# Dense queries and keys for the cross attention, and the delta rule's lower block applied to the scores

## What is computed

```python
# B=32 sequences, S=128 tokens, D=256.  x = LN(x + A(x)); x = LN(x + X(x, ctx)); x = LN(x + F(x))
# A: gated delta rule (4 key heads, 8 value heads of 128) and a mixture of 8 experts
q, k, v, z = split(zrms(x, w_ln1) @ W_qkvz)          # 512, 512, 1024, 1024 columns
beta = sigmoid(b); g = -exp(A_log) * softplus(a + dt_bias)
q, k, v = split(silu(causal_dwconv([q, k, v], conv_w)))   # 4 taps, q and k scaled to length 1
def step(S, inp):                                    # over the 128 tokens, per value head
    S = S * exp(gt)
    delta = (vt - kt @ S) * bt
    S = S + outer(kt, delta)
    o = qt @ S
core = rmsnorm(o) * gate_norm_w * silu(z)
h = x + core @ W_out
A(x) = h + sum over the 2 best of 8 experts of route * (silu(n @ Wg) * (n @ Wu)) @ Wd, n = zrms(h, w_ln2)
# X: cross attention, 16 heads of 16, over 128 context rows of the same sequence
scores = einsum('bnlh,bnph->bnlp', heads(x @ Wq.T + bq), heads(ctx @ Wk.T + bk)) / 4
scores = where(mask, scores, -1e8)
X(x, ctx) = (softmax(scores) @ heads(ctx @ Wv.T + bv)) @ Wo.T + bo
# F: 16 columns of 64 neurons, a gate that keeps one column, projection, layer norm
```

## Time and profile before

| | |
|---|---|
| median of 3 runs | 2331.67 us (2329.76 to 2333.71) |
| the profiled execution | 2329.89 us |
| its span | 2327.9 us |
| busy PE / PEld / DVE / ACT / POOL | 2219.2 / 1901.7 / 1678.1 / 1404.4 / 768.9 us |
| mean granted TensorE clock | 0.984 |
| DMA | 30.75 MB, nearly all of it in the first 40 us |

### The profile page before, as it was taken

One profiled execution on the slowest core, in us unless ns is written; L12 is line 12 of the kernel. 1 busy time (PEld: TensorE's weight loads), 2 busy tenths in 40 slices (PEclk: granted clock), 3 DMA queues, 4 the chain that ended last, 5 costly groups with the idle time before them and its releaser, 6 DMA issues.

```text
span 2327.9 us, 82936 instructions
## 1 busy us (share of the span) xinstructions
PE 2219.2 (95%) x33994; PEld 1901.7 (82%) x34026; DVE 1678.1 (72%) x5322; ACT 1404.4 (60%) x4326; POOL 768.9 (33%) x1771
## 2 busy tenths in 40 slices
PE   5899999999999999999999999999999999999986
PEld 4788888888888888888888888888888888888875
DVE  4577777777777777777777777777777777777753
ACT  3576555776555776555776555776555776555742
POOL 2332324333324332324332324333323333324321
PEclk8899999999999999999999999999999999999997
DMA  6000000000000000000000000000000000000000
GB/s 221 7 2 10 9 10 9 9 2 10 10 9 9 9 2 9 10 9 9 9 2 9 10 10 9 9 2 10 9 10 9 9 2 9 10 9 9 7 4 3
DMA packets 25065, 30.75 MB, mean 13 GB/s; under 512 B 8529, under 2 KB 21857, under 8 KB 23921
## 3 DMA queue, kind: packets, MB, share of 16 engines
q1 hardware_dynamic: 24688, 25.46, 3.3%
HBM read 21.25 MB, written 4.19 MB: 11 GB/s over the span
## 4 chain that ended last, share of the span: by engine, by line
PE 55%; DVE 22%; ACT 18%; issue 4%; POOL 1%; DVEq 0%; POOLq 0%
PE bank_b L644 10%; PE bank_a L460 6%; PE bank_b L736 5%; PE bank_b L652 5%; DVE acc L1010 4%; PE bank_a L542 4%; DVE diag L1046 3%; PE bank_b L673 3%; DVE y1p L1140 3%; DVE u L1087 3%; PE bank_a L581 3%; PE bank_a L572 3%; ACT prob L923 2%; ACT acc L814 2%; PE bank_a L532 2%
## 5 line engine op out<-in xcount | busy, mean ns | idle before, releaser
L1010 DVE SCALAR_TENSOR_TENSOR acc<-ypad,convw,acc 128x128 f32<-128x128 f32 x1536 | 432.2, 349 | 73.0 <-ACT acc L814 72.7
L460 PEld LDWEIGHTS bank_a<-xnT,wqkvz 128*128 128x128 f32 x2048 | 242.6, 195 | 43.3 <-DVE u L1087 42.8
L460 PE MATMUL bank_a<-xnT,wqkvz 128*128 128x128 f32 x2048 | 258.9, 281 | 17.1 <-DVE u L1087 17.1
L911 ACT ACTIVATE y1T<-bank_b 128x256 f32<-128x256 f32 x32 | 12.3, 384 | 313.0 <-PE bank_b L666 313.0
L1417 POOL TENSOR_SCALAR lnv<-mv 128x1 f32<-128x1 f32 x128 | 31.1, 243 | 509.5 <-DVE mv L1101 506.9
L923 ACT ACTIVATE prob<-bank_b,nmax 128x128 f32<-128x128 f32 x512 | 179.7, 374 | 2.2 <-DVE nmax L1160 1.8
L814 ACT ACTIVATE acc<-bank_a,convw 128x128 f32<-128x128 f32 x512 | 149.4, 405 | 0.0
L1321 POOL TENSOR_TENSOR gate<-ba,dtb 128x8 f32<-128x8 f32 x32 | 6.5, 203 | 430.3 <-ACT ba L825 430.3
L1158 DVE TENSOR_REDUCE smax<-bank_b 128x4 f32<-128x512 f32 x128 | 87.8, 686 | 68.5 <-PE bank_b L683 68.5
L736 PEld LDWEIGHTS bank_b<-y2T,wc 128*128 128x128 f32 x1024 | 124.3, 195 | 14.4 <-issue 14.4
L903 ACT ACTIVATE prob<-bank_b 128x512 f32<-128x512 f32 x64 | 38.2, 597 | 160.1 <-PE bank_b L644 160.1
(11 more groups left out here) (244 smaller groups left out, 5845.3 us busy)
## 6 DMA issues: line engine op xcount, KB each, us to landing
xin<-in_x_dram SPq DMA_DIRECT2D x32, 128.0 KB, 2.1
cin<-in_ctx_dram SPq DMA_DIRECT2D x32, 128.0 KB, 2.1
out_dram<-yout SPq DMA_DIRECT2D x32, 128.0 KB, 2.9
wqkvz<-in_wqkvz_dram SPq DMA_DIRECT2D x6, 512.0 KB, 6.8
wout<-in_wout_dram SPq DMA_DIRECT2D x1, 1024.0 KB, 9.8
wg<-in_wg_dram SPq DMA_DIRECT2D x1, 1024.0 KB, 11.4
wu<-in_wu_dram SPq DMA_DIRECT2D x1, 1024.0 KB, 13.4
wd<-in_wd_dram SPq DMA_DIRECT2D x1, 1024.0 KB, 15.2
```

Source lines behind the costliest of these rows:

```text
L460: last = mm(A[bank][:, b * P:(b + 1) * P], wqkvz[:, c, o:o + P], xnT[:, c, :], start=(c == 0), stop=(c == KC - 1))
L1010: stt(acc[:, c, :], ypad[:, c, k:k + P], convw[:, c, k:k + 1], acc[:, c, :], ALU.mult, ALU.add).then_inc(conv.sem, 1)
```

## The change

1. `q` and `k` are laid out dense: two heads share 32 rows, 128 rows hold 8 heads, so 2 blocks in place of 4. The keys stay in four blocks `kT`, in which `madj` (now 0 or 1 times mask) leaves one head of each pair and sets the other's rows to zero. Scores are 8 products with 256 moving columns (two key blocks side by side).
2. The mask row goes. Each score bank first gets `fill_bf` through a bf16 product with the identity, 512 columns, and the scores are added to it. POOL makes `madj` and `fill_bf` in three instructions where one was.
3. `a_w` and its DVE subtraction go. `a_mt` has 16 products where it had 8: the second set multiplies the lower inverse with the lower block of the scores. ACT writes the first result into `zfull` (negated), DVE the second into `scoreT` (`a_low`). `a_sz` now waits for both, ACT copies only its upper 64 rows back to `scoreT`, and `a_o` uses `scoreT`.
4. The arrays in DRAM stay padded. SP gathers the dense weights: 16 DMAs for `wq` and `wk` (128 partitions, 4 pieces of 16 floats each) and 32 for `bq` and `bk` (16 partitions, one float each), behind the 8 of `wo`; the four plain loads go. All count for `W_B`.
5. All four lists of `ORDER` are new.

```diff
-    put("mask_row", (p % 32 == HD) * -1.0)
+    put("parity", (p % 32 // HD == np.arange(2)[None, :]) * 1.0)
...
+    pe="b_v@2 b_x2T@2 a_lb01@1 a_la10@1 b_router@2 b_gu0@2 b_gu1@2 a_la11@1 a_lb10@1 b_gu2@2 a_la20@1 "
+       "a_lb11@1 b_gu3@2 b_dn0@2 a_lb20@1 a_la21@1 b_dn1@2 a_lb21@1 a_vT0@1 a_la30@1 b_k@2 a_la31@1 a_lb30@1 "
+       "a_lb31@1 b_y1T@2 a_pa@1 b_q@2 a_pb@1 c_s a_mt@1 c_pT0 a_vT1@1 a_xT a_sz0@1 c_pT1 a_ba a_qkv0 c_pT2 "
+       "a_o0@1 a_sz1@1 c_pT3 a_qkv1 a_o1@1 c_pv c_R a_z0 a_z1 c_xo a_qkv2 a_qkv3 c_y2T a_dec0 c_h a_ss c_lg "
+       "c_c0 a_st c_c1 c_wT a_kk c_spread a_dec1 c_pj0 b_oT0 b_oT1 c_pj1 b_w0 b_w1 a_la00 b_cT a_qk a_la01 "
+       "a_lb00".split(),
+    act="b_sum@2 b_cT@2 b_x2T@2 b_sg0@2 b_rl@2 b_sg1@2 b_rt@2 a_mix2@1 a_mix3@1 a_sum b_y1T@2 a_zf@1 b_q@2 "
+       "a_zo@1 c_exp0 a_mt@1 c_exp1 a_xT c_exp2 a_sz0@1 c_exp3 a_ba a_qkv0 a_o0@1 a_sz1@1 c_pT0 c_pT1 a_qkv1 "
+       "a_o1@1 c_R a_ln a_z0 a_mix0 a_z1 a_seg a_mix1 a_sq c_y2T c_h a_qkv2 a_st c_lt a_qkv3 c_c0 c_te c_wT "
+       "c_c1 a_dec0 a_dec1 b_oT0 b_oT1".split(),
+    dve="a_lb31@1 a_pa@1 b_k@2 a_u0@1 c_y4@3 c_max0 c_max1 a_xn c_max2 a_low@1 a_u1@1 c_max3 c_pT0 a_conv00 "
+       "a_conv01 c_pT1 a_conv02 c_rec a_core0@1 a_conv10 c_ao a_conv11 a_core1@1 c_sum2 a_conv12 c_y2 c_lb "
+       "c_route a_conv20 a_ss c_gc0 c_weight c_gc1 a_lower a_init c_sum3 b_hid a_la00 c_y3 b_x2 a_la01 "
+       "a_lb00 a_conv21 b_v a_conv22 a_lb01 a_conv30 a_la10 a_conv31 a_la11 a_lb10 b_act0 b_top a_conv32 "
+       "a_la20 a_lb11 a_score b_act1 b_ys0 a_la21 a_lb20 b_ys1 a_lb21 a_la30 a_la31 b_y1 a_lb30".split(),
+    pool="c_y2b@3 a_rq@1 c_ln2@3 b_xh@2 b_rs@2 b_rd@2 b_rt@2 c_ln3@3 a_xr@1 b_ln0@2 b_y1b@2 a_x a_osc0@1 a_ga "
+       "a_osc1@1 a_g c_ln1 c_rx b_mask c_sig a_sc".split(),
...
-        wq = sb("wq", [P, KC, 4 * P])
-        wk = sb("wk", [P, KC, 4 * P])
+        wq = sb("wq", [P, KC, 2 * P])
+        wk = sb("wk", [P, KC, 2 * P])
...
-        szT = decay
-        carryT = gseg[0:64, :, 0:64]
...
+        madj = sb("madj", [P, 2, P])
+        fill_bf = sb("fill_bf", [P, P], BF16)
...
+        dense_qk = [(w[:, :, P * o:P * o + P].rearrange("p k (j c d) -> p k j c d", j=4, c=2)[:, i, :, c, :],
+                     w_d.rearrange("p k (a j t) -> p k a j t", a=4, j=4, t=32)[:, i, 2 * o + c, :, 0:HD])
+                    for w, w_d in ((wq, wq_d), (wk, wk_d)) for i in range(KC) for o in range(2) for c in range(2)]
+        dense_b = [(b[32 * j + HD * c:32 * j + HD * c + HD, o:o + 1], b_d[32 * j:32 * j + HD, 2 * o + c:2 * o + c + 1])
+                   for b, b_d in ((bq, bq_d), (bk, bk_d)) for j in range(4) for o in range(2) for c in range(2)]
         W_A = 16 * (len(loads_a) + len(small_a))
-        W_B = 16 * (len(loads_b) + len(small_b) + len(dense_wo))
+        W_B = 16 * (len(loads_b) + len(small_b) + len(dense_wo) + len(dense_qk) + len(dense_b))
...
-            for dst, src in small_b + dense_wo:
+            for dst, src in small_b + dense_wo + dense_qk:
                 sp.dma_start(dst, src).then_inc(w_b.sem, 16)
+            for dst, src in dense_b:
+                sp.dma_start(dst, src, allow_slow_non_contiguous=True).then_inc(w_b.sem, 16)
...
-                    pe.wait_ge(*w_ok(n - 1, 1))
+                    pe.wait_ge(*carry_ok(n - 1))
...
-                    pe.wait_ge(*(w_ok(n - 1, 2) if g == 0 else core_ok(n - 1, 4 - g)))
+                    pe.wait_ge(*(lower_ok(n - 1) if g == 0 else core_ok(n - 1, 4 - g)))
...
             def a_mt(n):
+                pe.wait_ge(*score_ok(n))
                 pe.wait_ge(*zfull_ok(n)).then_inc(pe_passed.sem, 1)
                 for h in range(HV):
-                    last = mm(A[0][TOP, 64 * h:64 * h + 64], zfull[TOP, h, TOP], kkT[TOP, h, BOT], start=True, stop=True)
+                    part = slice(64 * h, 64 * h + 64)
+                    mm(A[0][BOT, part], kkT[TOP, h, BOT], zfull[TOP, h, TOP], start=True, stop=True)
+                    last = mm(A[3][BOT, part], zfull[BOT, h, BOT], scoreT[BOT, h, BOT], start=True, stop=True)
                 last.then_inc(carry_ps.sem, 1)
 
-            def solve_w(n, half):
+            def score_z(n, half):
                 pe.wait_ge(*carry_ok(n))
+                pe.wait_ge(*lower_ok(n))
                 pe.wait_ge(*u_ok(n, 1 + half)).then_inc(pe_passed.sem, 1)
-                for b in range(4):
-                    h = 4 * half + b
-                    last = mm(A[(0, 3)[half]][BOT, b * P:(b + 1) * P], carryT[:, h, :], u[TOP, h, :], start=True, stop=True)
-                last.then_inc(w_ps.sem, 1)
-
-            def score_z(n, half):
-                pe.wait_ge(*zfull_ok(n))
-                pe.wait_ge(*score_ok(n))
-                pe.wait_ge(*u_ok(n, 1 + half))
                 for b in range(4):
                     h = 4 * half + b
                     last = mm(A[1 + half][:, b * P:(b + 1) * P], zfull[:, h, :], scoreT[:, h, :], start=True, stop=True)
                 last.then_inc(sz_ps.sem, 1)
 
             def read(n, half):
-                pe.wait_ge(*sz_ok(n, 1 + half))
-                pe.wait_ge(*w_ok(n, 1 + half))
+                pe.wait_ge(*sz_ok(n, 1 + half)).then_inc(pe_passed.sem, 1)
                 for b in range(4):
                     h = 4 * half + b
-                    last = mm(A[1 + half][:, b * P:(b + 1) * P], szT[:, h, :], u[:, h, :], start=True, stop=True)
+                    last = mm(A[1 + half][:, b * P:(b + 1) * P], scoreT[:, h, :], u[:, h, :], start=True, stop=True)
                 last.then_inc(o_ps.sem, 1)
...
             def b_k(n):
                 pe.wait_ge(*ysum(n, 2))
-                for b in range(4):
+                for b in range(2):
...
             def b_q(n):
                 pe.wait_ge(*y1T_ok(n))
-                for b in range(4):
+                for b in range(2):
...
             def c_s(n):
-                pe.wait_ge(*q_ok(n))
-                pe.wait_ge(*k_ok(n))
-                for b in range(4):
+                pe.wait_ge(*madj_ok(n))
+                for j in (0, 2, 1, 3):
+                    if j == 1:
+                        pe.wait_ge(*k_ok(n))
+                    if j == 3:
+                        pe.wait_ge(*q_ok(n))
+                    mm(quad(Bk[j]), ident_bf[:, :], fill_bf[:, :].unsqueeze(1).to_broadcast([P, 4, P]), start=True, stop=False)
+                for o in range(2):
                     for j in range(4):
                         r = slice(32 * j, 32 * j + 32)
-                        last = mm(Bk[j][:, b * P:(b + 1) * P], qT[r, b, :], kT[r, b, :], start=True, stop=True)
-                        if b == 3:
+                        last = mm(Bk[j][:, D * o:D * o + D], qT[r, o, :], kT[r, 2 * o:2 * o + 2, :], start=False, stop=(o == 1))
+                        if o == 1:
                             last.then_inc(s_ps.sem, 1)
...
             def a_sq(n):
                 act.wait_ge(*mixed_ok(n, 2))
+                if not first(n):
+                    act.wait_ge(*o_ps(n - 1))
                 fn(sqk[:, :, :], mixed[:, 0:QK_BLOCKS, :], ACT.Square).then_inc(sq_ok.sem, 1)
...
                 act.wait_ge(*carry_ps(n))
-                fn(carryT, A[0][TOP, :].rearrange("p (h c) -> p h c", c=64), ACT.Copy).then_inc(carry_ok.sem, 1)
+                fn(zfull[BOT, :, TOP], A[0][BOT, :].rearrange("p (h c) -> p h c", c=64), ACT.Copy, scale=-1.0).then_inc(carry_ok.sem, 1)
 
             def score_z(n, half):
                 act.wait_ge(*sz_ps(n, 1 + half))
-                fn(heads(szT, half), quad(A[1 + half]), ACT.Copy).then_inc(sz_ok.sem, 1)
+                fn(scoreT[TOP, 4 * half:4 * half + 4, :], quad(A[1 + half])[TOP, :, :], ACT.Copy).then_inc(sz_ok.sem, 1)
...
                 act.wait_ge(*q_ps(n))
-                for b in range(4):
+                for b in range(2):
...
-            def solve_w(n, half):
-                dve.wait_ge(*w_ps(n, 1 + half))
-                tt(u[BOT, 4 * half:4 * half + 4, :], u[BOT, 4 * half:4 * half + 4, :], quad(A[(0, 3)[half]])[BOT, :, :],
-                   ALU.subtract).then_inc(w_ok.sem, 1)
+            def a_low(n):
+                dve.wait_ge(*carry_ps(n))
+                nc.vector.tensor_copy(scoreT[BOT, :, BOT], A[3][BOT, :].rearrange("p (h c) -> p h c", c=64)).then_inc(lower_ok.sem, 1)
...
                 dve.wait_ge(*madj_ok(n))
                 for b in range(4):
-                    last = stt(kT[:, b, :], Bk[1][:, b * P:(b + 1) * P], bk[:, b:b + 1], madj[:, :], ALU.add, ALU.mult)
+                    o, c = b // 2, b % 2
+                    last = stt(kT[:, b, :], Bk[1][:, o * P:(o + 1) * P], bk[:, o:o + 1], madj[:, c, :], ALU.add, ALU.mult)
...
             def b_mask(n):
+                if not first(n):
+                    pool.wait_ge(*s_ps(n - 1))
                 pool.wait_ge(*m_loaded(n)).then_inc(pool_passed.sem, 1)
-                ts(madj[:, :], m_u8[:, :], con("mask_row"), None, ALU.add).then_inc(madj_ok.sem, 1)
+                for c in range(2):
```

(2 more changed lines are left out.)

34 lines of the change are left out of this document (10 added, 24 removed), and 8 rows, old and new, of tables (dve, pe).

## The result

The kernel with the change took 2308.4 us (median of 7 runs, 2303.1 to 2319.6), the kernel before beside it 2329.8 (2327.9 to 2333.7): ratio 0.9907, interval 0.9885 to 0.9928. It is faster, by 21 us where 47 were forecast. The profiled execution took 2305.4, its span 2303.6, so the spans differ by 24.3.

The account below looks back on a forecast made before the run. PE, busy 95% of the span, was taken as the bound. 2329.9 - 73.6 (32 periods, 2.3 us each) + 24.8 (start) = 2281.1, which with 1.8 to the median gave 2283 us; forecast's own range 2267 to 2312, whole range 2245 to 2320.

Parts of the forecast that it names:

- PE's work: PE's steps per period: -3.95 removed, +0.84 fills, +0.30 a_mt, scores unchanged; sum -2.81 us, between -4.15 and -0.85.
- The waits: PE's idle time per period under the new orders: 0.8 + 0.3 - 0.6 = +0.5 us, period falling 2.3 to 67.9.
- (1): Behind the scores: c_pT0 waits for ACT's exponentials with only a_mt (about 1.4) ahead; up to 1.0 us idle, 0.8 taken.
- (2): Ahead of b_y1T: expert sum and normalisation need 4.2 us, filler is 3.7; idle 0.5 against 0.2.
- (3): At a_qkv2: it waited 0.49 us for a_core through a chain mostly on ACT; 0.5 of idle left as is.
- 0.6 of old gaps: Smaller old PE gaps that the new list closes, taken off the added idle: 0.6 us a period.
- The start: Once, at trip 2: PE stands until the last gathered weight or bias lands, 70.5 - 45.7 = 24.8 us; bounds 14 and 70.
- Rival (a): At the start: gather pieces cost 0.125 us each or more; 2329 us, no gain, or 2393 at twice that; chance 0.04.
- (c): The start is cheap, 14 us down to 7; time 2265 to 2272 us; chance 0.16.
- (e): Scores of 256 columns lose row-group overlap; 2325 us at half the loss, 2366 at all; chance 0.02.
- (d): New order closes old gaps: period falls 3.4, 2248 us, or 2238 if a_mt's second set is free; chance 0.14.
- (b): Waits eat the work: PE idles 0.8 more a period, a_mt sets don't overlap (+0.8); 2334 or 2356 us; chance 0.08.

Follow-up runs that it names:

- e3: The kernel before with c_pT0 moved ahead of a_sz0 and a_sz1 in PE's list, same work; 2389.8 us, ratio 1.026 to the kernel before.
- e9: e1 plus three useless float products (256 columns ahead of b_k, 128 behind b_y1T, 512 ahead of c_pT0); 2286.8 us, ratio 0.981 to the kernel before.
- e2: The changed kernel plus five useless bf16 products of 512 columns in front of c_pT0's wait; 2313.3 us, ratio 0.992 to the kernel before.
- e7: e1 plus one useless float product of 512 columns in front of c_pT0's wait; 2288.7 us, ratio 0.982 to the kernel before.
- e8: e1 with a_vT1 in front of c_pT0 instead of behind it; 2291.8 us, ratio 0.985 to the kernel before.
- e14: e13 with DVE's a_low moved behind the first maximum, no useless work; 2286.0 us, ratio 0.982 to the kernel before.
- e15: e1 plus two useless float products (256 columns ahead of b_k, 128 behind b_y1T); 2295.7 us, ratio 0.985 to the kernel before.
- e1: The changed kernel with dense query and key weights in DRAM, four plain loads replacing the 48 small ones; 2292.4 us, ratio 0.984 to the kernel before.
- e13: e1 with a_vT1 moved from behind c_pT0 to behind b_k, into the 0.45 us wait; 2296.4 us, ratio 0.987 to the kernel before.

## Why the forecast was wrong

The sign was right and so were the kinds of gain and loss that the forecast named; the size was off by half, since the idle per period was put too low and two things were missing, the chain that bounds the new period and the falls of the clock. Of the profiled execution's span, -48.8 was forecast and -24.3 measured. The periods gave 16.6 us too little before any disturbance: 13.2 from 30 periods that fell by 1.86 and not by 2.3, 3.4 because 32 periods were priced where 30 and a remainder of 1.2 us stand; the disturbances took 17.3, and the start gave 9.4 back: 16.6 + 17.3 - 9.4 = 24.5.

**PE's work: near, partly by luck.** Forecast -2.81 a period, measured -3.25. Counted from each step's start to the next one's in the two undisturbed periods, the steps that the forecast named gave only -2.65: `b_k` takes 1.16 us for 1.98, `b_q` 1.09 for 1.98, `a_w` (1.96) is gone, the fills take 0.97 (0.84 forecast), the scores 1.08 for 1.10, `a_mt` 1.15 for 1.07. Two of them saved less than was forecast, the fills cost more, and `a_mt` made up for half of it: both sets, 32 records, ran from 1580.14 to 1581.29. The second set is nearly free: the two halves of the array's rows ran side by side, the lower bound of the forecast's range, 0 where +0.30 was taken. The other 0.6 us came from steps that the change left alone and the forecast held constant, the value transposes (-0.29), the diagonal levels (-0.11) and some projections among them. They stand next to other steps in the new order; that this is the cause was not tried. The forecast's bound of -4.15 is too low by its own terms: with the fills at 0.84 it is -3.31.

**The waits: the step that failed first.** "So added idle is ... +0.5" was +1.40. (1) `c_pT0` waits 1.43, not 0.8. The exponentials' end was right (2.4 us behind the scores' end at 1580.2), but what lies ahead of the wait is 1.1 us of `a_mt`, not 1.4, and the 0.2 that I gave back for an earlier table load weren't there, since the first exponential waits for DVE's maximum. An overlap that makes PE's work cheaper lengthens the wait behind it by as much. (2) `b_y1T` doesn't wait in an undisturbed period; the same lateness of the expert sum shows at the steps around it, 0.45 at `a_la31` and 0.27 at `a_pa`. (3) The 0.49 at `a_qkv2` is gone; L463 waited 2.0 us in all. (4) The "0.6 of old gaps" was too generous: the window of the earlier trace rows was a period of 70.23 with 1.77 idle, where the shortest has 69.53 and 1.32. I should have compared all periods before taking one as typical. That the period came out at 67.67 where 67.9 was forecast is luck: a base 0.7 too long and 0.4 too little work saved stood against 0.9 too little idle.

**What bounds the period: a step that was missing.** The forecast let PE's work and waits add up, which held for before (e3 pays its wait in full). After the change it holds no more: e9 adds 1.75 us of PE work for nothing. What ends last is a chain across engines: last `b_dn`, DVE's expert sum and normalisation, `b_y1T`, the transposed queries on ACT, `b_q`, the scores, DVE's maximum, ACT's exponentials, `c_pT0`. That it is this chain is read from the trace; that PE's idle time is slack is shown by e2, e7, e8 and e9.

**The disturbances: not in the forecast at all.** It took the clock as full because the earlier trace rows showed 1.00. 17.3 us of the missing 24.5 are here. In the 29 full periods the amount on top rose by 18.0 us (9.5 to 27.5), 15 of it busy time of PE and 3 idle. The busy part goes with the products at 1.2 GHz (the fills above, 1.89 us for 1.04), the idle part with stalls and the waits behind them. That falls come where PE has been idle, and go when such a wait is closed, is shown by e3, e9, e14 and e15; why one such place brings a fall and the next doesn't is open. So is why 1.43 us at `c_pT0` brings none in after, and 1.5 at the same step brings 8 in e3.

**The start: mechanism right, size wrong.** Forecast 24.8, measured 15.4 and, by e1, 16.0. `wo` was issued by 34.0 (34.5 forecast), the biases took 15.2 (15.0). The gather took 5.26 + 4.36 = 9.6 us, 0.60 a DMA, not 1.15: the extrapolation from 128 and 256 pieces to 512 didn't hold, and the lower bound (7.5) was the nearer. The last issue ended at 58.98, ACT and PE go on at 60.1. Rival (a) falls: from issue to landing the gathers took 3.0 and 2.4 us in the median, hardly longer than the context's 2.1:

```profile
wq<-in_wq_dram SPq DMA_DIRECT2D x8, 32.0 KB, 3.0
wk<-in_wk_dram SPq DMA_DIRECT2D x8, 32.0 KB, 2.4
```

The last of `wk` was issued by 43.7, so by about 46 all of them had landed, when PE had been waiting for about 1 us (60.14 less 15.07 is 45.07). What kept it standing until 60 were the 32 bias loads behind them, 2 KB in all. The Trainium skill's rule on pieces under 512 B (DMA: Bandwidth & Descriptors, Specifications) shows no price in this kernel's start.

**The rivals.** Nothing of (c) to (e) came alone: the start was nearly as cheap as in (c) (15.4 us for 7 to 14), the second `a_mt` set free as in (d), the scores kept their overlap against (e). (b) named the right kind of loss, waits that eat the work, at 0.8 a period; measured are 0.9 more idle than forecast. Of the signs, "`a_mt` near 1.4", "`c_pT0` 0.8", "`b_y1T` 0.5" and "1.15 us" were wrong, PE busy (64.95 for 65.6) and the period (67.67 for 67.9, mean 68.5) near.

## What to carry to other kernels

When one engine is busy 95% and over and you take work off it, price the waits first: walk the cross-engine chain that the removed work covered, and take the period from the longer of the two, the engine's list or the chain. Move steps on all engines together, and look for useful work to put into each new gap. Lay the granted clock and the idle places of TensorE over all periods, of before and of after: three falls of after behind waits of 0.45 to 0.79 and 0.27 us made their periods 1.2 to 3.0 us longer than the 67.95 of those without fall or stall. And a tiny load costs its issuer nearly as much as a larger one (0.47 us for 64 bytes, 0.60 for 32 KB): lay such rows out in DRAM so that one load takes them.

## What the runs showed of the hardware

- The granted clock of TensorE fell to half for 3.4 to 10.2 us at a time, in periods in which it is otherwise nearly always busy. Around the start of each of the 118 falls TensorE had been idle for 0.54 us or more; with a wait of 0.27 us behind one of 1.43 four falls began there (e13), without it none (e14), and one wait of 1.5 us (e3) brought 8 where before had none.
- TensorE stands still for 0.6 to 1.8 us with no semaphore to wait for, 1 to 11 times in 30 periods. Each of the stops of before and after over 0.6 us (9 in all) ended 2.2 to 2.9 us behind the start of a 16 KB packet of the instruction queue; the one at 1713.77 is such. Of the 247 such packets in the 30 periods of after, 6 stand ahead of such a stop. The DMA part of the trace for 1711 to 1714 us of after:

```profile
DMA packets 1, 0.02 MB, mean 5 GB/s; under 512 B 0, under 2 KB 0, under 8 KB 0
...
q8 instruction: 1, 0.02, 1.9%
```

  That it waits for its own instructions there is likely and was not tried.
- A DMA of 512 pieces of 64 bytes (128 rows by 4) costs its issuer 0.60 us, one of 16 values of 4 bytes, one to a row, 0.47. The first kind landed 2.4 to 3.0 us behind its issue.
